# The causal mask of the row maxima: added by a product on TensorE, or by VectorE in the instruction that takes the maximum

## The reference

```python
attn = jnp.einsum('bhtl,bsl->bhts', q_lat, c_kv) / math.sqrt(hs)
causal_mask = jnp.triu(jnp.ones((T, T), bool), k=1)
attn = jnp.where(causal_mask[None, None], -jnp.inf, attn)
attn = jax.nn.softmax(attn, axis=-1)
```

## Time and profile before

| | |
|---|---|
| three runs, median | 2015.13 us (2012.6 to 2019.75) |
| the profiled execution | 2020.24 us, span 2018.4 us, mean granted clock 0.924 |
| TensorE busy (matmul) | 1729.3 us, 86%, 10685 matmuls |
| VectorE busy | 1465.3 us, 73%, 1473 instructions |
| ScalarE, POOL busy | 1327.9 us (66%), 886.2 us (44%) |
| mask products L372 | 256, from 1308.9 to 1616.0 us |
| maxima of the second attention | 256 of the 512 of L579, from 1310.3 us |

### The profile page before, as it was taken

How to read it: one execution, slowest core, us unless ns; L and a number is a source line. 1 busy time by engine, 2 the same in 40 slices (tenths; PEclk the granted TensorE clock), 3 DMA queues, 4 the chain that set the end, 5 groups by cost and what they waited for, 6 DMA issues and landing times. The chain is left out here.

```text
span 2018.4 us, 32287 instructions
## 1 busy us (share of the span) xinstructions
PE 1729.3 (86%) x10685; PEld 762.3 (38%) x10685; DVE 1465.3 (73%) x1473; ACT 1327.9 (66%) x2673; POOL 886.2 (44%) x567
## 2 busy tenths in 40 slices
PE   6779999999887676677777689989999989999996
PEld 2223333333344343444444334334444444233332
DVE  3677888888299999999999954476666624465456
ACT  4427777777799999989999734436656653553433
POOL 1065566655099999999999910000000010000000
PEclk8759999999988899898988899989999998999998
DMA  2354444443498888988888620312122000000000
GB/s 109 127 175 153 152 163 153 163 153 127 150 322 317 306 306 305 308 279 311 305 300 310 217 84 11 69 47 35 25 32 42 2 18 0 0 0 0 0 6 16
DMA packets 83730, 282.58 MB, mean 140 GB/s; under 512 B 11415, under 2 KB 12722, under 8 KB 82079
## 3 DMA queue, kind: packets, MB, share of 16 engines
q1 hardware_dynamic: 69503, 230.27, 34.7%
q0 software_dynamic: 13824, 50.34, 6.5%
q10 hardware_dynamic: 288, 0.45, 0.1%
HBM read 214.60 MB, written 61.21 MB: 137 GB/s over the span
## 5 line engine op out<-in xcount | busy, mean ns | idle before, releaser
L1662 POOL TENSOR_TENSOR hc<-st,ct 128x1024 f32<-128x1024 f32 x256 | 598.2, 2377 | 5.1 <-DVE st L1621 4.9
L579 DVE TENSOR_REDUCE attn_mx<-banks 128x1 f32<-128x1024 f32 (+7 forms) x512 | 498.0, 988 | 135.1 <-PE banks L372 84.3
L1621 DVE TENSOR_TENSOR_SCAN st<-da,banks 128x1024 f32<-128x1024 f32 x256 | 562.1, 2265 | 14.5 <-ACT da L1578 5.6
L531 ACT ACTIVATE attn_probs<-banks 128x512 f32<-128x512 f32 (+3 forms) x640 | 312.2, 534 | 167.6 <-PE banks L406 84.8
L1586 ACT ACTIVATE ut<-b_turned,mats 128x128 f32<-128x128 f32 x1024 | 311.7, 387 | 1.7
L1578 ACT ACTIVATE da<-dt,mats 128x1024 f32<-128x1024 f32 x256 | 282.5, 1138 | 24.2 <-DVE st L1621 17.8
L402 PE MATMUL banks<-attn_qa,attn_ka 75*128 75x512 bf16 (+3 forms) x896 | 279.3, 367 | 7.9 <-DMA attn_qa<-attn_mrow 6.2
L1503 PE MATMUL banks<-hc,onecol 128*32 128x512 f32 x1024 | 159.3, 698 | 107.8 <-POOL onecol L1660 83.6
L370 PE MATMUL banks<-attn_ka,attn_qa 64*128 64x512 bf16 (+4 forms) x640 | 210.9, 365 | 29.1 <-DVE attn_mx L579 25.5
L757 POOL TENSOR_TENSOR made_ahead<-b_turned,x_turned 128x1024 f32<-128x1024 f32 x96 | 183.8, 1914 | 113.5 <-DVE attn_mparts L594 67.0
L1479 PE MATMUL banks<-mats,ut 128*128 128x128 f32 x1024 | 158.7, 298 | 38.3 <-DVE st L1621 29.8
(11 more groups left out here) (442 smaller groups left out, 1962.9 us busy)
## 6 DMA issues: line engine op xcount, KB each, us to landing
dt<-dt_rows SPq DMA_DIRECT2D x256, 512.0 KB, 5.5
ahead<-made_ahead POOLq DMA_DIRECT2D x96, 512.0 KB, 3.5
ua<-ahead SPq DMA_DIRECT2D x96, 512.0 KB, 5.8
attn_qa<-q_lin SPq DMA_DIRECT2D x144, 64.0 KB
attn_ka<-k_lin SPq DMA_DIRECT2D x72, 64.0 KB
attn_qu<-attn_qa SPq DMA_DIRECT2D x8, 512.0 KB, 4.3
moe_w<-in_moe_w SPq DMA_DIRECT2D x2, 2048.0 KB, 10.9
mats<-in_mats SPq DMA_DIRECT2D x1, 2876.5 KB, 12.9
```

The source lines that it names most:

```text
L531: nc.scalar.activation(probs[s % 4][:, jj, c0:BLK], scores_exp[jj][:, c0:BLK], ACT.Exp, scale=scale).then_inc(probs_ready, 1)
L579: nc.vector.reduce_max(mx[:, qt, j:j + 1], scores_max[n % 2][:, 0:w], AX.X)\
L1621: nc.vector.tensor_tensor_scan(st[n % 4][:, :], da[n % 4][:, :], pair[:, :, :].rearrange("p h t -> p (h t)"), 0.0, ALU.mult, ALU.add).then ...
L1662: nc.gpsimd.tensor_tensor(hc[n % 8][:, :], st[n % 4][:, :], ct[:, b * SEQ:(b + 1) * SEQ], ALU.mult)\
```

## The change

The product L372 goes. In its place a constant `mask_wide` holds, for 128 queries, 896 columns of zero and then the 128x128 mask; its last `w` columns are the whole mask of a unit of width `w`. VectorE's reduction becomes one call that adds this to the scores, writes the sum back over them in PSUM, and gives the maximum. The first attention keeps the plain reduction. POOL clears the 896 columns, and VectorE waits once for the constants.

```diff
-    CONSTS = 3 if causal else 1
+    CONSTS = 4 if causal else 1
...
-        mask_qk = k.sb(f"{tag}_maskqk", [128, 128], BF16, ctx)
+        mask_wide = k.sb(f"{tag}_maskwide", [128, SEQ], BF16, ctx) if causal else None
...
-                    nc.gpsimd.tensor_copy(mask_qk[:, :], k.m("mask_qk")).then_inc(const_ready, 1)
+                    nc.gpsimd.memset(mask_wide[:, 0:SEQ - TILE], 0.0).then_inc(const_ready, 1)
+                    nc.gpsimd.tensor_copy(mask_wide[:, SEQ - TILE:], k.m("mask_qk")).then_inc(const_ready, 1)
...
-                        ins = nc.tensor.matmul(out[:, lo:hi], lhs, rhs, start=True, stop=not diag)
-                        if diag:
-                            ins = nc.tensor.matmul(out[:, w - TILE:w], ident_b[:, :], mask_qk[:, :], start=False,
-                                                   stop=True)
+                        ins = nc.tensor.matmul(out[:, lo:hi], lhs, rhs, start=True, stop=True)
...
-                    nc.vector.reduce_max(mx[:, qt, j:j + 1], scores_max[n % 2][:, 0:w], AX.X)\
-                        .then_inc(max_taken, 1)
+                    out = scores_max[n % 2][:, 0:w]
+                    if causal:
+                        nc.vector.tensor_tensor_reduce(out, out, mask_wide[:, SEQ - w:SEQ], 1.0, -BIG, ALU.add, ALU.max,
+                                                       mx[:, qt, j:j + 1]).then_inc(max_taken, 1)
+                    else:
+                        nc.vector.reduce_max(mx[:, qt, j:j + 1], out, AX.X).then_inc(max_taken, 1)
...
                 front.vector_first(dve)
+                dve.wait_ge(const_ready, CONSTS)
```

More of the change, by code:

```diff
@@ L362, in max_unit @@
                         hi = min(lo + BLK, w)
-                        diag = causal and hi == w
                         if causal:
```

## The result

The changed kernel took 2029.95 us (median of 8, 2023.62 to 2040.02) where the kernel before, timed beside it, took 2018.72 us (8, 2012.18 to 2025.94): a ratio of 1.0065 with the interval [1.0038, 1.0092]. It is slower, by 11 us between the medians and 13 by the ratio, where 5.6 us less were forecast; put on the forecast's base of 2015.13 us the ratio gives 2028.2 us, 9 us beyond the range. The profiled execution took 2029.37 us, with a mean granted clock of 0.915 against 0.924 before. Every ratio here takes in only runs within 1.5% of the quickest of the same kernel, which leaves runs out in experiments 9 and 10 alone.

The account below looks back on a forecast made before the run. TensorE was taken to bound the passes, VectorE the lead-in. Removed mask products gave -8.8 us, added reads +3.2, together -5.6 from 2015.13, so 2009.5 us; range 2004 to 2019.

Parts of the forecast that it names:

- the DMA wait: Sign in each pass: TensorE's wait for the DMA of the turned maxima goes from 0.6 to about 0.9 us.
- the wait at unit (1,0): Sign at the next pass's start: TensorE's wait for unit 31's maximum goes from 1.2 to about 1.3 us.
- r: Time each maximum's added read on VectorE costs: 0.08 us, ends -0.016 and 0.26, counted 40 times on the path.
- -1.20 + 0.24: Change per pass: 21 of 32 removed mask products on the path save 1.20 us, three reads add 0.24.
- -0.4 + 19 r: Lead-in: four removed masks on the path save 0.4 us, 19 added reads on the chain cost r each.
- TensorE, with less to do in the lead-in, is granted the lower level for longer: Clock rival, lead-in: up to 6 us more, giving 2015 to 2016 us; chance 0.04.
- in the passes TensorE stays over 90% busy: Argument against the clock being granted lower for longer, given for the passes; no size of its own.
- a fixed 0.057 us: Price of each removed 128-column mask product on TensorE, from the distance between starts of four in a row.
- The read is overlapped: Denies a rival for VectorE's maxima: read not overlapped, r 0.15 to 0.26, result -2.7 to +1.6 us; chance 0.22.
- The read isn't free: Denies a rival for VectorE's maxima: read free, r near 0, result -8.8 us, 2006.3 us; chance 0.10.
- Two cycles: Rival: VectorE's sum with running maximum takes two cycles a column, VectorE becomes the bound, 2090 us; chance 0.04.
- fixed cost over the 0.37 us: Rival: some fixed cost above 0.37 us in VectorE's new instruction, +6 us and more; chance 0.04.

Follow-up runs that it names:

- experiment 9: Kernel before without the mask product, plain reduction kept, three unread products added in the lead-in only: 2013.53 us, ratio 0.9977 to the kernel before.
- experiment 10: Changed kernel run again unaltered: ratio 1.0048 to the kernel before, from the eight quickest of 14 runs; median of all 14 2040.65 us.
- experiment 1: Changed kernel with the 128-column mask product put back on TensorE, VectorE's sum kept: 2024.65 us, ratio 1.0021 to the kernel before.
- experiment 7: Kernel before without the mask product, plain reduction kept, unread products in the passes' waits and lead-in: 2008.46 us, ratio 0.9938 to the kernel before.
- experiment 4: Changed kernel with unread products in TensorE's waits of the passes and three more in the lead-in: 2010.62 us, ratio 0.9956 to the kernel before.
- experiment 5: Kernel before with the same unread products in the passes' waits and lead-in as experiment 4: 2017.78 us, ratio 0.9995 to the kernel before.
- experiment 6: Changed kernel with only the three unread products of the lead-in, none in the passes: 2025.73 us, ratio 1.0033 to the kernel before.
- experiment 3: Changed kernel with unread TensorE products in the waits of the passes, none added in the lead-in: 2016.09 us, ratio 0.9986 to the kernel before.
- experiment 2: Kernel before without the mask product, plain reduction kept, so no mask in the maxima: 2020.7 us, ratio 1.0002 to the kernel before.
- experiment 8: Experiment 4 with seven unread products instead of two at the last pass's DMA wait: 2009.25 us, ratio 0.9941 to the kernel before.

## Why the prediction was wrong

**The mechanism of the instructions was right.** A pass of 37.78 us where 37.8 was forecast; the DMA wait 0.8 (0.9), the wait at unit (1,0) 1.25 (1.3), r = 0.06 (0.08), and 3 r = 0.18 us a pass in experiments 1 and 7. Experiments 4 and 5 give the whole second attention at an even clock: from the first unit to the experts 338.54 us against 345.14, -6.6. The six steps from pass to pass (-5.90) and the last pass (-0.90) make -6.8 of that, where seven times -1.20 + 0.24, -6.7, were forecast; the rest is the lead-in, +0.2, where -0.4 + 19 r = +1.1 were forecast. That term isn't settled by these traces: with the same instructions in it the lead-in took 38.40 us in experiment 6 and 38.76 in experiment 4. At an even clock the forecast would have been 1 to 2 us off.

**The failing step is the clock**, in the part on the rivals: "TensorE, with less to do in the lead-in, is granted the lower level for longer", priced at "up to 6 us" there, with 0.04, and set aside for the rest by "in the passes TensorE stays over 90% busy". The rival came true in the profiled lead-in (+5.07 us), though not always, as experiment 3 shows. What failed is the reason for leaving the passes out. TensorE did stay over 90% busy, its share of a pass going from 36.41 of 38.75 us, 94.0%, to 34.93 of 37.78, 92.5%; but that did not keep its clock, and it was granted the lower level, 0.50, for a part of two passes of the profile, in which its longest wait was 1.3 us, for VectorE, and the longest for a DMA 0.8 us. The kernel before itself gave a hint: it already holds unread products in the lead-in and in pass 0. The sum priced every removed product at a fixed 0.057 us and so treated TensorE's speed as given. In fact the products removed were part of what held it: with products that nobody reads in the waits, the time falls from a ratio of 1.0065 to 0.9956, 22 us of 2019, while no wait gets longer.

**What the other rivals come to.** The read is overlapped: it starts 0.08 us before the main record ends, and adds 0.06. The -2.7 us at the near end of that rival has the read's whole record behind the main one, -8.8 + 40 x 0.153, and the 0.153 was an estimate from L2872; no run shows such a term. The 0.05 us for a longer start, in the high end of 0.26, is the difference in the kernel before between 512 columns of a SCALAR_TENSOR_TENSOR with the column operand `cols` (738 ns, L960) and without it (692 ns, L1301); the new instruction takes 11 ns more than the old at 1024 columns and 18 more at 128 (304 against 286), so nothing of that size was added. The read isn't free. Twice the time for a column is out: 1233 ns for 1024 columns, where the scan L1621 takes 2265. "Two cycles" there stands for that doubling, an estimate of the author from those rows; no trace here shows VectorE's cycle, and what is measured is (1222 - 286) / 896 = 1.04 ns a column before and (1233 - 304) / 896 = 1.04 in the new instruction. There was no fixed cost over the 0.37 us asked about, and ScalarE and the DMA ate no more than forecast (waits of 0.2 and 0.8 us in the pass).

**The spread of the kernel before** is wide too: beside experiments 1 to 8 it ranged from 2011.38 to 2032.26 us over 66 runs, and the 7 us between the three runs shown ahead had been taken for noise of the measurement. In the two profiles at hand it does not come from the passes, which keep their clock: the spans of the kernel before and of experiment 5 are 7.8 us apart, 2.7 of it ahead of the second attention and 5.8 behind it, in code that both share.

**What stays open.** In the profile identical passes got different clocks (37.02 and three times 37.78 to 37.80 us, then 44.94 and 40.83), so what decides on a fall is not in the view of a pass that I have; I found no rule for it. Nor is it shown why six of the 14 runs of experiment 10 were so much longer than the eight of the result. Whether the 0.06 us on VectorE really add some 8 us by way of the clock (experiments 6 and 9) stays open, and if so, why: its direct effect on TensorE is only that some waits are 0.06 us longer. And whether the three products in the lead-in are needed, or those in the passes alone would do, can't be told: 0.9986 without and 0.9956 with them have intervals that overlap, and the lead-in was at full clock in both profiles.

## What to carry to other kernels

Before taking small work off TensorE, ask what fills its place. Here waits grew in part of it (from 0.6 to 0.8 us for the DMA, from 1.18 to 1.25 us at unit (1,0)), and the removal cost more in clock than it saved in work: two steps with a fall +8.28 us, four without -3.97. The price of one instruction times their count is only the gain at an even clock. Look at the granted clock stretch by stretch in passes of equal content; where one of them is longer at the same count of matmuls, put unread products into the waits and time that, before judging the change itself. Do the same to the kernel before, so that what is compared is the change and not the clock (experiments 4 and 5: -7.2 us, where the plain comparison gave +11 by the medians).

## What the runs showed of the hardware

- The granted clock fell from 1.00 to 0.50 in passes whose work keeps TensorE busy 92.5% of the time at 1.00, and which have no wait of it over 1.3 us; it cost 7.16 us in one pass (44.94 us at a mean of 0.77 against 37.78 at 1.00, changed kernel).
- Unread products of TensorE inside waits of 0.8 and 1.25 us cost nothing: six of them a pass left it at 37.78 us, and cut the waits shown there to 0.9 us in two and 0.3 us for the DMA (experiment 4).
- The same instructions of one lead-in ran at 0.50 in one trace (changed kernel, 1337 to 1349 us) and at 1.00 in another (experiment 3, 1337 to 1348 us).
- VectorE's sum with a running maximum over a PSUM and a bf16 SBUF input takes 1233 ns for 1024 columns, where the maximum of one input takes 1222. Its read has a record of 142 ns, and the next long instruction starts together with it (both at 1334.67), so in a row of maxima it adds 0.05 us each: 0.92 us from start to start at 768 columns, against 0.87 before (five reductions, one of 896 and four of 768 columns, in 4.55 us from 1333.43, less the last one's record of 1.08).
